# A four-layer graph kernel: the adjacency matrix is kept as two fp16 parts instead of being split again in each layer

## The chip, the cores and the metric

The kernel runs on one core of a Trainium2 chip. The time is the device time of one execution in microseconds (us), and a version's time is the median of its runs. The profile is of one execution, and its span is the time from that execution's first to its last instruction.

## The reference

`x` is 4096x128, `adj` is 4096x4096, both fp32. `adj` has about 0.2% of its entries and the diagonal set, and each row is divided by its count. Four layers follow each other, each with a residual and a layer norm:

```
x = LN(x + L0(x, adj))   XW = mobius(W, x); g = 2/(1-|XW|^2); (adj @ (g*XW)) / (adj @ (g-1)), then row-wise artanh, tanh
x = LN(x + L1(x, adj))   d^-1/2 (adj + I) d^-1/2 @ x @ W.T + b
x = LN(x + L2(x, adj))   dis*adj*dis @ x - x + sigmoid(alpha) * (softmax(beta * cos(x, x) * adj) @ x - x)
x = LN(x + L3(x, adj))   m = relu(adj @ x @ Wm.T + b); GRU cell of m and x
```

So `adj` (64 MB) multiplies a 4096x128 matrix four times, and layer 2 forms a second 4096x4096 matrix of attention weights.

## The kernel before

TensorE needs `adj` with the contracted index on the partitions, so `adj` must be turned. The work is cut into 8 slabs of 512 rows (`SLABS`), each into 32 blocks of 128 columns; two blocks are a pair, four are a group. The fp32 products are made in the format fp32r in three parts: an operand v is split into a high part (a copy rounded to fp32r) and a low part (v minus high), and high x high, high x low and low x high are added up.

**Layer 0.** For each of the 128 pairs: SP loads a tile (`load_tile`), TensorE turns 8 squares into a PSUM strip (`turn0`, two strips, run `AHEAD` = 4 pairs ahead), ScalarE copies the strip to SBUF (`full0`, a ring of 3 groups) and from there makes the high part (`high0`), VectorE subtracts to get the low part (`low0`), and TensorE multiplies both parts, as weights, with `Y` (`multiply0`, 16 products, 8 of 260 columns and 8 of 130). SP stores the turned fp32 strips in `adj_t` in DRAM. The result of a slab lands in four PSUM banks; `read_acc0` takes it out at the fourth pair of the next slab, and `rows0` does the row-wise arithmetic of a slab (scale, artanh, tanh, layer norm; some 40 small steps listed in `ROWS[0]`, spread over ScalarE, VectorE and GpSimd, each waiting for the one before by a semaphore) during the next slab. `Y` itself is also split in two parts: ScalarE's `y_high`, GpSimd's `y_low`.

**Layers 1 and 3.** SP loads groups of `adj_t` (`load_group`, 6 places, 1 MB each); for each pair ScalarE makes the high part (`high`, L857) and VectorE the low part (`low`, L1446), and TensorE makes 6 products of 512 columns (`multiply`, L541, L542, L550). The first 32 pairs take slabs 0 and 1 in turns (`TURNS`), because the last groups of `Y` come late. Row work (`rows1`, `rows3`) follows each slab. It puts small fp32 products on TensorE. The identity of layer 1 is added by four products with `eye`.

**Layer 2.** TensorE makes the scores of 32 row blocks (`score`, fp16, 3 products per half unit), VectorE multiplies them by `adj` (`mask`, which loads `adj` again in units of 0.5 MB), ScalarE takes the exponentials and scales them. 39 steps behind, TensorE turns the weights block by block (`turn2`), VectorE adds `dis` times the block of `adj_t` (`mix`, L1528), ScalarE and GpSimd (some on VectorE) split the sum (`high2`, `low2`), and TensorE makes 3 products (`multiply2`, L619 to L622).

**What sets the order.** Each engine's program is a written list and runs strictly in order; semaphores tie them. Row work is placed between pairs at fixed positions (`ROWS_FROM`, `HOOKS`, and leads `ACT_LEAD`, `DVE_LEAD`). All loads and the `adj_t` stores are in SP's queue, in order. There, the units that overwrite `x_nat` (places 22 to 25) wait until all of layer 2's `Y` is ready, and what stands behind them waits too.

Of the kernel before, what the change touches and what calls it, by code (L numbers as in the profile page):

```python
# [7 lines left out]
F32R = mybir.dt.float32r  # L8
# [25 lines left out]
LOADS = 14  # L34

# [3 lines left out]
AHEAD = 4  # L39
FULL_SLOTS = 3  # L40
# [41 lines left out]
KEPT_SLOTS = 4  # L82
# [4 lines left out]
     "floor_clip", "artanh_a", "artanh_b", "ratio", "h4", "log", "dcol", "dis", "series", "differ", "choose",  # L87
# [23 lines left out]
def build(nc, x, adj, w0, w1, b1, alpha, beta, w_msg, b_msg, w_ih, w_hh, b_ih, b_hh, out, scratch, dis_out):  # L111
    with ExitStack() as ctx:
# [6 lines left out]
        adj_t = nc.dram_tensor("adj_t", (SLABS, P, NB, SLAB), F32, kind="Internal").ap()  # L119
# [16 lines left out]
        Y = sb("Y", [P, NB, YW], F32R)  # L136
        part_h = sb("part_h", [P, 8, SLAB], F32R)
        part_l = sb("part_l", [P, 8, SLAB], F32R)
# [4 lines left out]
        turned_in = arena[:, TILE:FULL].rearrange("p (n w) -> p n w", w=Q * SLAB)  # L143
        full = arena[:, FULL:XNAT].rearrange("p (n w) -> p n w", w=Q * SLAB)
# [33 lines left out]
        dcol = sb("dcol", [P, NB])  # L178
        dis = sb("dis", [P, NB])
# [10 lines left out]
        scal = sb("scal", [P, 7])  # L190
# [5 lines left out]
        consts = sem("consts")  # L196
        dve_link = sem("dve_link")
# [24 lines left out]
        full_done = sem("full_done")  # L222
        stored = [sem(f"stored{n}") for n in range(FULL_SLOTS)]
# [5 lines left out]
        y_hi = sem("y_hi")  # L229
        y_ready = sem("y_ready")  # L230
# [46 lines left out]
        def parts_free(l, n):  # L277

            return product_base[l] if n < 4 and l > 1 else product_base[l] + n - 3
# [12 lines left out]
        def low_by_dve(b):  # L292
            return b in BY_DVE

        def low_at(l, n):
            if l == 2 and low_by_dve(n):
                return low_by_turns, BY_DVE.index(n) + 1
            skipped = len(BY_DVE) if l == 3 else sum(i < n for i in BY_DVE) if l == 2 else 0
            return low_done, product_base[l] + n - skipped + 1
# [1432 lines left out]
```

## Time and profile before

| what | value |
|---|---|
| median of 3 runs | 1412.92 us (1411.5 to 1417.08) |
| span of the profiled execution | 1412.7 us (no time of it is given apart from the span) |
| TensorE, VectorE, ScalarE, GpSimd busy | 93%, 77%, 75%, 41% of the span |
| DRAM read and written | 340 MB and 71 MB, 291 GB/s over the span |
| a copy of a 128x1024 strip, PSUM to SBUF, ScalarE (L802) | 1.01 us |
| four row squares with their sums, ScalarE (L833, L846) | 1.2 us; four relu (L841) 1.25 us; a change of function table 1.28 us |
| powers of 128x4 on GpSimd (L1096, L1098, L1103, L1106) | 1.0 to 1.1 us each |
| two wide GpSimd operations before the statistics (L1109, L1111) | 1.16 and 2.15 us |
| statistics of four blocks, VectorE (L1344 to L1351) | 1.4 us; four scalings (L1358) 1.1 us |
| two readouts of `acc0`, VectorE | 0.8 us |
| load of 0.5 MB of `adj` (L408), issue to landing | 5.9 us median |

A line of the windows view gives the stretch and its length, then for TensorE's products, its weight loads, VectorE, ScalarE and GpSimd the busy us and the number of instructions, then the granted TensorE clock as a share of full speed, the busy share of the 16 DMA engines, and GB/s. A line of a timeline gives start, length, engine, line of code, operation, result and operands; in brackets how long the engine was idle before it and what ended that. Products are pipelined, so the distance between starts is what one costs, not its length.

### The profile page before, as it was taken

The numbers are of one execution on the slowest core, as the hardware profiler recorded it, in microseconds if no ns is written. First come the engines' busy times: TensorE is split into PE (matmuls) and PEld (weight loads), VectorE is DVE, ScalarE is ACT, GpSimd is POOL, SyncE is SP. The second block draws the span as 40 slices with busy tenths as digits, with TensorE's granted clock in tenths as the row PEclk, the third lists the DMA queues.
The fourth block names the chain that finished last, engine by engine and source line by source line (L and its number), as shares of the span: only waits on it lengthen the run. The fifth ranks groups of instructions, "written<-read, shape, count | busy, mean of one in ns | idle before, by whom it ended". The sixth has DMA issues, their size and how long they took to land.

```text
span 1412.7 us, 21062 instructions
## 1 busy us (share of the span) xinstructions
PE 1308.7 (93%) x7640; PEld 1016.7 (72%) x7640; DVE 1085.0 (77%) x1946; ACT 1059.0 (75%) x1367; POOL 579.1 (41%) x441
## 2 busy tenths in 40 slices
PE   6999999999988989998799999999999879999996
PEld 5999999999986767773466666666666658767664
DVE  6856556555767989998888887988888878787885
ACT  6887888788777667775688879788798547767764
POOL 4312222222563543343477767777776650000010
PEclk9999999999989999999899999999999999999998
DMA  9999999999967878893678778788786849877860
GB/s 310 408 370 361 332 359 376 330 347 353 352 234 252 314 255 323 327 375 148 254 276 307 267 268 318 264 295 293 248 315 219 280 174 403 321 273 261 291 222 22
DMA packets 114824, 413.08 MB, mean 292 GB/s; under 512 B 10016, under 2 KB 23584, under 8 KB 90144
## 3 DMA queue, kind: packets, MB, share of 16 engines
q1 hardware_dynamic: 106528, 407.67, 79.3%
q10 hardware_dynamic: 8192, 4.06, 1.0%
q8 instruction: 60, 0.98, 0.3%
q14 instruction: 44, 0.36, 0.1%
HBM read 340.40 MB, written 71.30 MB: 291 GB/s over the span
## 4 chain that ended last, share of the span: by engine, by line
PE 53%; DVE 19%; ACT 16%; issue 7%; POOL 5%; DMA 1%; POOLq 0%; ACTq 0%; DVEq 0%; SPq 0%
DVE part_l L1446 6%; PE strip_b L605 5%; PE acc L550 5%; PE acc L541 4%; PE acc L542 4%; PE acc L522 3%; PE mid L522 3%; ACT arena L802 3%; PE acc L622 3%; PE strip_b L502 2%; DVE part_l L1325 2%; PE acc L619 2%; PE acc L620 2%; ACT part_h L857 2%; PE strip_a L502 2%
## 5 line engine op out<-in xcount | busy, mean ns | idle before, releaser
L1446 DVE TENSOR_TENSOR part_l<-arena,part_h 128x1024 fp32r<-128x1024 f32 x256 | 327.4, 1314 | 60.8 <-ACT part_h L857 59.4
L1150 POOL TENSOR_TENSOR part_l<-arena,part_h 128x512 fp32r<-128x512 f32 x237 | 304.4, 1298 | 151.0 <-ACT part_h L895 151.0
L857 ACT ACTIVATE part_h<-arena 128x1024 fp32r<-128x1024 f32 x256 | 265.7, 1057 | 125.6 <-PE acc L550 116.5
L1325 DVE TENSOR_TENSOR part_l<-arena,part_h 128x1024 fp32r<-128x1024 f32 x128 | 160.9, 1266 | 121.9 <-ACT part_h L809 121.1
L895 ACT ACTIVATE part_h<-arena 128x512 fp32r<-128x512 f32 x256 | 157.9, 625 | 94.8 <-DVE arena L1528 94.2
L541 PE MATMUL acc<-part_h,Y 128*128 128x512 f32 x512 | 222.2, 434 | 4.3 <-DVE arena L1333 2.1
L542 PE MATMUL acc<-part_h,Y 128*128 128x512 f32 x512 | 204.6, 400 | 0.0
L1118 POOL TENSOR_TENSOR sc<-sc,power 128x4 f32<-128x4 f32 x31 | 48.4, 1560 | 318.5 <-DVE sc L1351 318.5
L605 PEld LDWEIGHTS strip_b<-ident,arena 128*128 128x128 f32 x1024 | 126.1, 142 | 71.5 <-DVE arena L1528 20.1
L550 PE MATMUL acc<-part_l,Y 128*128 128x512 f32 x512 | 165.6, 405 | 10.3 <-DVE part_l L1446 10.1
L605 PE MATMUL strip_b<-ident,arena 128*128 128x128 f32 x1024 | 156.1, 275 | 18.8 <-DVE arena L1528 11.7
L809 ACT ACTIVATE part_h<-arena 128x1024 fp32r<-128x1024 f32 x128 | 135.8, 1061 | 35.5 <-PE mid L522 33.2
L522 PE MATMUL acc<-Y,part_h 128*128 128x260 f32 x496 | 143.3, 340 | 0.0
L522 PE MATMUL mid<-Y,part_h 128*128 128x260 f32 x496 | 142.7, 338 | 0.0
L884 ACT ACTIVATE arena<-arena,neg_peak 128x2048 f32<-128x2048 f32 x64 | 127.5, 1993 | 5.3 <-DVE neg_peak L1498 5.3
L520 PE MATMUL acc<-Y,part_l 128*128 128x130 f32 x512 | 126.4, 247 | 0.0
L550 PEld LDWEIGHTS acc<-part_l,Y 128*128 128x128 f32 x512 | 95.6, 191 | 39.2 <-DVE part_l L1446 18.4
L541 PEld LDWEIGHTS acc<-part_h,Y 128*128 128x128 f32 x512 | 98.2, 192 | 35.3 <-issue 7.9
L619 PE MATMUL acc<-part_h,Y 128*128 128x512 f32 x256 | 122.1, 477 | 0.0
L542 PEld LDWEIGHTS acc<-part_h,Y 128*128 128x128 f32 x512 | 98.0, 191 | 29.3 <-issue 9.1
L890 ACT ACTIVATE arena<-arena,weight 128x2048 f32<-128x2048 f32 x57 | 113.6, 1994 | 6.2 <-DVE weight L1512 6.2
L520 PE MATMUL mid<-Y,part_l 128*128 128x130 f32 x512 | 115.9, 226 | 0.0
(296 smaller groups left out, 2782.2 us busy)
## 6 DMA issues: line engine op xcount, KB each, us to landing
arena<-adj_t SPq DMA_DIRECT2D x128, 1024.0 KB, 4.9
arena<-in_adj SPq DMA_DIRECT2D x64, 1024.0 KB, 8.8
adj_t<-arena SPq DMA_DIRECT2D x64, 1024.0 KB, 8.0
arena<-in_adj SPq DMA_DIRECT2D x128, 512.0 KB, 5.9
part_h<-adj_t SPq DMA_DIRECT2D x64, 512.0 KB, 5.1
part_l<-adj_t SPq DMA_DIRECT2D x64, 512.0 KB, 5.1
scratch<-v ACTq DMA_DIRECT2D x8, 256.0 KB, 10.6
arena<-scratch SPq DMA_DIRECT2D x8, 256.0 KB, 5.3
```

Of the source, the lines that this page charges most:

```text
L520: last = pe.matmul(acc0[q][:, 0:LO], part_l[:, slot, mine], Y[:, j, 0:LO], start=False, stop=False)
L522: last = pe.matmul(acc0[q][:, 0:YW], part_h[:, slot, mine], Y[:, j, :], start=False, stop=stop)
L541: pe.matmul(to, Y[:, j, 0:D], h, start=j == 0, stop=False)
L542: pe.matmul(to, Y[:, j, LO:LO + D], h, start=False, stop=False)
L550: last = pe.matmul(to, Y[:, j, 0:D], part_l[:, 2 * (n % 4) + j % 2, :], start=False, stop=j == NB - 1)
L605: last = pe.transpose(strip_b[:, b % 2, P * q:P * (q + 1)], unit_in[:, place, P * (j % 8):P * (j % 8 + 1)], ident[:])
L619: pe.matmul(to, Y[:, j, 0:D], part_h[:, b % 4, :], start=j == 0, stop=False)
L857: act.activation(flat(part_h[:, slot:slot + 2, :]), turned_pair(n), ACT.Copy).then_inc(high_done, 1)
L895: act.activation(part_h[:, b % 4, :], mixed[b % G_SLOTS], ACT.Copy).then_inc(high_done, 1)
L1150: pool.tensor_tensor(part_l[:, b % 4, :], mixed[b % G_SLOTS], part_h[:, b % 4, :].bitcast(F32), ALU.subtract).then_inc(low_done, 1)
L1325: dve.tensor_tensor(flat(part_l[:, slot:slot + 2, :]), full_pair(n), flat(part_h[:, slot:slot + 2, :]).bitcast(F32), ALU.subtract).then_in ...
L1446: dve.tensor_tensor(flat(part_l[:, slot:slot + 2, :]), turned_pair(n), flat(part_h[:, slot:slot + 2, :]).bitcast(F32), ALU.subtract).then_ ...
```

## The change

`adj_t` becomes fp16 and holds for each block the high part and the low part of 1024 x `adj`, so its size stays. The copy `full0` goes: ScalarE's `high0` and VectorE's `low0` read the PSUM strip and write the two fp16 parts into a ring of 7 groups, from which TensorE multiplies and SP stores. `AHEAD` is 2, and a strip is free when `low0` has read it. Layers 1 and 3 multiply the loaded parts; `high` and `low` are gone there. In layer 2 `mix` takes only the high part of `adj_t`, and a fourth product multiplies the low part with `Y_dis`, a new fp16 matrix (`dis` times x). `Y` is fp16 too. Scale factors keep fp16 in range. `y_low` of layers 2 and 3 becomes two GpSimd instructions, in layer 2 `y_with_dis` is a third; in layer 0 `y_low0` is on VectorE, and `sum_parts` and `sum_den` move from GpSimd to VectorE. Two steps, `dcol_y` and `dis_y`, are added to `ROWS[0]` on GpSimd.

```diff
-AHEAD = 4
-FULL_SLOTS = 3
+A_SCALE = 1024.0
+AHEAD = 2
+RING_SLOTS = 7
-KEPT_SLOTS = 4
+KEPT_SLOTS = 6
...
-        adj_t = nc.dram_tensor("adj_t", (SLABS, P, NB, SLAB), F32, kind="Internal").ap()
+        adj_t = nc.dram_tensor("adj_t", (SLABS, GROUPS, P, Q * 2 * SLAB), F16, kind="Internal").ap()
-        Y = sb("Y", [P, NB, YW], F32R)
+        Y = sb("Y", [P, NB, YW], F16)
+        Y_dis = sb("Y_dis", [P, NB, D], F16)
...
# SP: stores, reloads of a pair for layer 2
-                    sp.wait_ge(full_done, 2 * n + 2)
+                    sp.wait_ge(low_done, 2 * n + 2)
+                    sp.dma_start(adj_t[s, c], ring_slot(n)).then_inc(stored[n % RING_SLOTS], 16)
-                    sp.wait_ge(mixed_done, 2 * (n - KEPT_SLOTS) + 2)
+                    sp.wait_ge(product, product_base[2] + 2 * (n - KEPT_SLOTS) + 2)
...
# TensorE: turn0, multiply (layers 1 and 3), multiply2
-                    pe.wait_ge(full_done, n - 1)
+                    pe.wait_ge(low_done, n - 1)
+                    high, low = pair[:, j % 2, 0, :], pair[:, j % 2, 1, :]
+                    pe.matmul(to, Y[:, j, 0:D], high, start=j == 0, stop=False)
+                    pe.matmul(to, Y[:, j, LO:LO + D], high, start=False, stop=False)
+                    last = pe.matmul(to, Y[:, j, 0:D], low, start=False, stop=j == NB - 1)
...
+                pe.matmul(to, Y_dis[:, j, :], kept_slot(b // 2 % KEPT_SLOTS)[:, b % 2, 1, :], start=j == 0, stop=False)
...
# ScalarE
-            def full0(n):
-                act.activation(full_pair(n), flat(strip[n % 2][:]), ACT.Copy).then_inc(full_done, 1)
             def high0(n):
-                act.activation(flat(part_h[:, slot:slot + 2, :]), full_pair(n), ACT.Copy).then_inc(high_done, 1)
+                if g >= RING_SLOTS:
+                    act.wait_ge(*held_stored(g - RING_SLOTS))
+                    act.wait_ge(product, 2 * (g - RING_SLOTS) + 2)
+                act.activation(ring_pair(n)[:, :, 0, :], strip[n % 2][:], ACT.Copy, scale=A_SCALE).then_inc(high_done, 1)
...
-                high(1, n)
-                high(3, n)
...
# GpSimd
             def y_low(l, g):
+                source = mx[:, rows_, :]
+                if l > 1:
+                    pool.wait_ge(y_ready, SLABS * l + g)
+                    source = turned[0][:].rearrange("p (q d) -> p q d", d=D)
+                    pool.tensor_scalar(source, x_nat[:, rows_, :], Y_SCALE, 0.0, ALU.mult, ALU.add).then_inc(x_scaled, 1)
+                    pool.wait_ge(x_scaled, SLABS * (l - 2) + g + 1)
+                pool.tensor_tensor(Y[:, rows_, LO:LO + D], source, Y[:, rows_, 0:D], ALU.subtract).then_inc(y_ready, 1)
+            def y_with_dis(g):
+                pool.tensor_tensor(Y_dis[:, rows_, :], x_nat[:, rows_, :], wide(dis_y[:, rows_]), ALU.mult)
...
                 if 6 <= n < 6 + GROUPS:
+                    y_with_dis(n - 6)
                     y_low(2, n - 6)
...
# VectorE
+            def y_low0(g):
+                dve.scalar_tensor_tensor(Y[:, rows_, LO:LO + D], Y[:, rows_, 0:D], -Y0_LOW, mx[:, rows_, :],
+                                         ALU.mult, ALU.add).then_inc(y_ready, 1)
             def low0(n):
+                dve.scalar_tensor_tensor(pair[:, :, 1, :], strip[n % 2][:], A_SCALE, pair[:, :, 0, :],
+                                         ALU.mult, ALU.subtract).then_inc(low_done, 1)
-                low(1, n)
-                low(3, n)
```

## Rows read from the trace of the kernel before

**Rows 1.** windows of the four layers; columns as in the section on the profile
```profile
38.00:418.50 380.50, 360.51 (x3035) 354.89 (x3033) 228.22 (x475) 309.82 (x451) 112.31 (x90) 0.97 0.94 348
418.50:641.50 223.00, 208.79 (x934) 163.90 (x935) 200.23 (x301) 152.73 (x194) 90.28 (x51) 0.97 0.83 308
641.50:1150.00 508.50, 474.19 (x2584) 304.26 (x2582) 430.20 (x838) 395.75 (x468) 345.09 (x276) 0.99 0.76 267
1150.00:1390.00 240.00, 231.99 (x916) 167.40 (x917) 189.55 (x244) 168.76 (x204) 13.55 (x10) 0.99 0.72 265
```

**Rows 2.** timeline of TensorE in layer 1 (start, us, what); five products lie between
```profile
571.27 0.39 PE L541 MATMUL acc<-part_h,Y 128*128 128x512 f32 x1
...
572.66 0.39 PE L541 MATMUL acc<-part_h,Y 128*128 128x512 f32 x1
```

**Rows 3.** timeline of TensorE in layer 2, around one block
```profile
866.73 0.60 PE L605 MATMUL strip_b<-ident,arena 128*128 128x128 f32 x4
867.08 0.47 PE L619 MATMUL acc<-part_h,Y 128*128 128x512 f32 x1
867.40 0.39 PE L620 MATMUL acc<-part_h,Y 128*128 128x512 f32 x1
...
868.09 0.38 PE L589 MATMUL strip_a<-arena 128*128 128x512 f16 x1
868.30 0.38 PE L590 MATMUL strip_a<-arena 128*128 128x512 f16 x1
```

**Rows 4.** timeline of TensorE in layer 0: transposes of successive pairs
```profile
85.16 1.04 PE L502 MATMUL strip_b<-ident,arena 128*128 128x128 f32 x8
...
87.88 1.03 PE L502 MATMUL strip_a<-ident,arena 128*128 128x128 f32 x8
```

**Rows 5.** chain that ended last: like marks, six slabs apart, then one slab apart
```profile
86.51 1.23 DVE part_l L1325
...
371.80 1.23 DVE part_l L1325
...
765.81 1.28 DVE arena L1487
...
825.85 1.28 DVE arena L1487
```

**Rows 6.** a window of layer 0 with dense transfers
```profile
50.00:55.00 5.00, 5.00 (x46) 5.00 (x45) 5.00 (x4) 4.56 (x6) 2.66 (x2) 1.00 1.04 416
```

**Rows 7.** timeline of SP's queue where layer 3 begins
```profile
1145.93 20.01 SPq L424 DMA_DIRECT2D arena<-scratch  x2
```

**Rows 8.** groups by line: count, busy us, mean ns, idle before and its releaser
```profile
L809 ACT ACTIVATE part_h<-arena 128x1024 fp32r<-128x1024 f32 x128 | 135.8, 1061 | 35.5 <-PE mid L522 33.2
...
L520 PEld LDWEIGHTS acc<-Y,part_l 128*128 128x128 f32 x512 | 100.7, 197 | 0.0
...
L1528 DVE SCALAR_TENSOR_TENSOR arena<-part_l,dis,strip_b 128x512 f32<-128x512 f32 x128 | 93.8, 742 | 9.0 <-PE strip_b L605 4.8 <-DMA part_l<-adj_t 3.5 <-issue 0.5
...
L588 PEld LDWEIGHTS strip_a<-arena 128*128 128x128 f16 x128 | 12.4, 97 | 41.0 <-issue 29.2 <-DVE peak L1487 10.5
```

**Rows 9.** timeline of VectorE in slab 0 of layer 0, two like instructions
```profile
34.03 0.69 DVE L1319 TENSOR_TENSOR arena<-arena,v 128x512 f32<-128x512 f32 x1
...
35.77 1.76 DVE L1319 TENSOR_TENSOR arena<-arena,v 128x512 f32<-128x512 f32 x1
```

**Rows 10.** timelines of GpSimd, SP, VectorE where layer 2 begins, one line group
```profile
650.18 1.04 POOL L1146 TENSOR_TENSOR v<-arena,sc 128x512 f32<-128x512 f32 x1
651.18 9.89 POOL L1078 TENSOR_TENSOR Y<-arena,Y 128x512 fp32r<-128x512 f32 x8
...
661.10 5.68 SPq L408 DMA_DIRECT2D arena<-in_adj  x9
...
672.56 1.28 DVE L1487 CUSTOM_DVE_ANT_0 arena<-strip_a,arena,scal 128x1024 f32<-128x1024 f32 x1
...
L1168 POOL TENSOR_SCALAR v<-v,scal 128x512 f32<-128x512 f32 x8 | 5.6, 694 | 0.1
```

More of the change, by code:

```diff
@@ L34 @@
 LOADS = 14
-AHEAD = 4
-FULL_SLOTS = 3
+A_SCALE = 1024.0
+Y0_SCALE = 0.25
+Y0_LOW = 2048.0
+Y_SCALE = 256.0
+WHOLE = A_SCALE * Y_SCALE
+AHEAD = 2
+RING_SLOTS = 7
 TURNED_SLOTS = 6
@@ L293, in low_by_dve, with low_at @@
             return b in BY_DVE
[L295 to L299, printed above, removed]
+        def low_at(b):
+            if low_by_dve(b):
+                return low_by_turns, BY_DVE.index(b) + 1
+            return low_done, split_done(b) - sum(i < b for i in BY_DVE)
         def unit_loads(k):
@@ L403, in load_unit @@
                         last = (GROUPS * SLABS - 1 - slot) // TURNED_SLOTS * TURNED_SLOTS + slot
-                        sp.wait_ge(low_done, product_base[1] + 2 * last + 2)
+                        sp.wait_ge(product, product_base[1] + 2 * last + 2)
                     else:
@@ L517, in multiply0 @@
                         mine = slice(P * q, P * (q + 1))
+                        high, low = pair[:, j % 2, 0, mine], pair[:, j % 2, 1, mine]
                         if start:
-                            pe.matmul(acc0[q][:, 0:YW], part_h[:, slot, mine], Y[:, j, :], start=True, stop=False)
-                        last = pe.matmul(acc0[q][:, 0:LO], part_l[:, slot, mine], Y[:, j, 0:LO], start=False, stop=False)
+                            pe.matmul(acc0[q][:, 0:YW], high, Y[:, j, :], start=True, stop=False)
+                        last = pe.matmul(acc0[q][:, 0:LO], low, Y[:, j, 0:LO], start=False, stop=False)
                         if not start:
-                            last = pe.matmul(acc0[q][:, 0:YW], part_h[:, slot, mine], Y[:, j, :], start=False, stop=stop)
+                            last = pe.matmul(acc0[q][:, 0:YW], high, Y[:, j, :], start=False, stop=stop)
                 last.then_inc(product, 1)
@@ L824, in read_acc @@
                     act.wait_ge(row[s % 2], row_base(1, s))
-                act.activation(to, acc[:, s % 2, :], ACT.Copy).then_inc(acc_read, 1)
+                act.activation(to, acc[:, s % 2, :], ACT.Copy, scale=1.0 / WHOLE).then_inc(acc_read, 1)
             def rows0(k, s):
@@ L1101, in rows0 @@
                     pool.tensor_tensor(dcol[:, mine], sc[:, DEG, :], sc[:, KEEP, :], ALU.mult).then_inc(row[par], 1)
+                    before("dcol_y")
+                    pool.tensor_scalar(dcol_y[:, mine], dcol[:, mine], Y_SCALE, 0.0, ALU.mult, ALU.add).then_inc(row[par], 1)
                     before("dis")
                     pool.tensor_tensor(dis[:, mine], sc[:, ZERO, :], inv_half[:, 0:Q], ALU.pow).then_inc(row[par], 1)
+                    before("dis_y")
+                    pool.tensor_scalar(dis_y[:, mine], dis[:, mine], Y_SCALE, 0.0, ALU.mult, ALU.add).then_inc(row[par], 1)
                 if k == 20:
@@ L1371, in rows0 @@
                 total = nat[:, :, D + 1]
+                if k == 7:
+                    before("sum_parts")
+                    dve.wait_ge(acc_read, acc_reads_done(0, s))
+                    dve.scalar_tensor_tensor(t_of[par][:], nat[:, :, LO:LO + D], 1.0 / Y0_LOW, nat[:, :, 0:D],
+                                             ALU.mult, ALU.add).then_inc(row[par], 1)
+                    before("sum_den")
+                    dve.scalar_tensor_tensor(val(DEN), nat[:, :, LO + D], 1.0 / Y0_LOW, nat[:, :, D],
+                                             ALU.mult, ALU.add).then_inc(row[par], 1)
                 if k == 8:
@@ L1646, in _ @@
                 low0(n)
+                if s == 0 and 1 <= m <= GROUPS:
+                    y_low0(m - 1)
                 if s > 0:
```

190 lines of the change are left out of this document (90 added, 100 removed).

## The prediction

> **What bounds the kernel now.** I read the stages first, then in each the engine that is never idle, then what it waits for. [rows 1] cut the span at the layer boundaries: layer 0 takes 380.5 us, layer 1 223, layer 2 508.5, layer 3 240, the tail 22.7. TensorE is busy 94 to 97% of each, so the spacing of its instructions decides most of it. In layers 1 and 3 the reader is to see six fp32r products of 512 columns per pair of blocks in 1.39 us (0.232 each, [rows 2]). In layer 2 one block takes 0.35 for four transposes, 0.32 for the first product, then 0.23 each, while the fp16 score products follow at 0.215 [rows 3]. Layer 0 takes 2.72 us per pair when nothing waits [rows 4]; that is about 0.8 of transposes (0.35 for four, [rows 3]) and 1.9 for 16 short products. But six of its slabs take 285.3 us between like marks, 47.5 each [rows 5], which is 4 us more than 16 x 2.72: the row work of the slab before holds ScalarE up. A slab of layer 2 takes 60.04 us [rows 5], 2.4 more than 32 blocks of 1.80.
>
> **Layer 1.** The split of `adj` goes: one 1.06 us ScalarE and one about 1.3 us VectorE instruction per pair, 128 times each in this layer, so that no compute engine feeds TensorE. What is late next is TensorE itself, since 6 fp16 products take 6 x 0.2155 = 1.293 us. A slab is 16 x 1.293 = 20.7 plus 2.1 for 20 small fp32 products (eye, weight, unit) at about 0.1, as four transposes take 0.35 in [rows 3], 22.8 us. A slab of transfers is 8.39 MB; at the 416 GB/s of [rows 6] it takes 20.2 us, so it stays hidden, by 2.6 us per slab. Sum: 8 x 22.8 = 182.4, 1 to start, and about 5 at the start for the last row work of layer 0 and for `x_bias` of slabs 1 and 2: the former is a chain like that of the next paragraph but one with `Y` behind it, about 33 us, and pair 28 (28 x 1.293 = 36) needs its end. 189 against 223: **-34**, bounds -24 to -44.
>
> **Layer 3.** The same saving per pair is 0.1 us; its row work is TensorE's own and stays. 116 pairs after the first 12 give -12. The first 12 have their data early; the next groups wait in SP's queue behind the reload of the last `scratch` slab, which held it for 20 us [rows 7]. That slab's layer norm no longer shares VectorE with four 1.2 us subtractions, so SP goes on some 3 us earlier: **-15**, bounds -6 to -20.
>
> **Layer 0.** ScalarE loses one of two 1 us copies per pair. Products get half-width weights: the load takes 97 ns instead of 197 [rows 8], and two loads of about 0.117 make the 0.235 us in which a product of 130 and one of 260 columns follow each other. With fp16 390 columns at 2.4 GHz take 0.163; I take 0.175, so a pair costs 0.8 + 8 x 0.175 = 2.2 us instead of 2.72 (bounds 2.1 and 2.72). This would be 35 us a slab. It is not what I predict, because the strip now holds more: `AHEAD` falls from 4 to 2, and a strip is free only when VectorE too has read it. So TensorE's transposes of pair n+2 wait for `low0(n)`, and what is queued behind `high0` and `low0` on ScalarE and VectorE is the row work of the slab before, 42 steps with hand-overs. I added up that row work between `low0` of pair 4 and of pair 15 from the small durations in the table of the profile section and 0.2 for each step on VectorE, with 1.06 for `high0` [rows 8] and 1.22 to 1.28 for `low0` (0.742 for 512 columns from PSUM [rows 8] and 512 more at the same rate). Pair 4: 3.6 us (low, degrees, then a wait of 1.3 for four squares); pair 5: 3.4 (two powers on GpSimd); 6: 1.7; 7: 3.2 (Ln, then four GpSimd instructions where two stood; the new two of 128x4 I take at 0.3 each, between nothing and the 0.69 of a 128x512 one, [rows 10]); 8: 2.0; 9 and 10: 4.9 (relu, squares, power, tanh); 11: 4.0; 12: 4.9 (3.3 on GpSimd before the statistics); 13: 3.2; 14 and 15: 1.2 each. This makes 33.3. At the slab's end TensorE turns pair 18, and its first product waits until high0(18), low0(18) and the readout behind them are done (1.06 + 1.28 + 0.8 + hand-overs, 3.3 us), a stall that 4 pairs ahead had covered. From low0(14) to the next low0(4): two pairs of 2.2, 1.0, 3.3, 1.4, one pair of 2.2, a transpose group of 1.0 and 1.1, 14.4 us. Slab: 33.3 - 1.2 + 14.4 = 46.5 against 47.5. Sum over seven slabs -7. In slab 0 the subtraction of `Y` leaves GpSimd, which had slowed VectorE's `y_scale` from 0.69 (the first, when GpSimd was idle) to 1.77 [rows 9]; low, scale and the new `y_low0` make 2.65 a pair against 2.83, and 2.2 for the rest: -3 with the new stall at its end. **-10**, bounds -40 and +15.
>
> **Layer 2, begin.** GpSimd now prepares `Y` in three instructions per group instead of one. Before, eight took 9.9 us [rows 10]. Now each group is 1.04 (like the product with a wide operand), 0.69 (tensor_scalar) and 1.24, with hand-overs 3.1, so 24.6: `y_ready` is 14.7 us later. SP stops for it and then issues nine units and the first pairs, as it did at 661.1. The first of those units is used by the mask at 672.6 [rows 10]; it would land at 661.1 + 14.7 + 5.9 (such a load's median, in the table) = 681.7. So the cover of 672.6 - 661.1 - 5.9 = 5.6 us is used up and **+9** is left (bounds +3 and +14). SP's queue also has the pairs behind it: first pair at 675.8 + 10 x 0.524 MB / 0.41 + 2 = 690.6, when the first mix is ready for it.
>
> **Layer 2, steady.** One product more per block, 0.2155. Three others shorten by 0.017, and the first after the transposes by 0 to 0.1. TensorE's block becomes 1.86 to 1.95, I take 1.895, +0.095 or 3.0 per slab. A part of the 2.4 us of waits shrinks, as the other engines gain 3 us of slack per slab: +2.2 a slab over 6.8 slabs. **+15**, bounds 0 and +32. In the last 39 steps (no scores) VectorE and GpSimd set the pace; six times 0.75 us more on GpSimd in that chain: **+3** (0 to +5). Pairs are reloaded only after their product, but with 6 places instead of 4, so a load is asked for at the same step.
>
> **Sum.** -34 - 15 - 10 + 9 + 15 + 3 = -32. The profiled execution spans 1412.7, the median of the runs is 1412.92 and I know of no time of that execution outside its span. Prediction 1381.
>
> *Two rules of the Trainium skill.* The 416 GB/s of [rows 6] is above what the Trainium skill ("DMA: Bandwidth & Descriptors", Specifications) calls the limit of HBM for one core, about 358 GB/s; by that rule a slab of layer 1 would take 8.39 / 0.358 = 23.4 and one of layer 0 46.9, some 8 us more in all; this trace disagrees in all its dense stretches. The fp16 products of 512 columns follow at 0.215 in [rows 3]; "TensorE: Matmul & The Clock Gate" of the Trainium skill (Back-to-back issue gap) gives about 131 ns in a sustained stream, by which layer 1 would be bound by transfers at 20.2 a slab, 21 us less, 1360 in all; the rows disagree, and I give it 0.02.
>
> **Rivals.** (B) The waits of layer 0 hide each other, and transfers become its bound: 16.78 MB a slab at 0.41 is 41 us, 5.5 less than I have, seven times: 1381 - 38 = 1343. For it: ScalarE has 1 us less per pair. Against it: the chain is serial across three engines. 0.15. (C) Transfers of layers 0 and 1 don't hold 410 GB/s beside TensorE's faster pace (most of layer 0 shows 350 to 380): at 358 it costs 8: 1389. 0.1. (D) Layer 2 pays in full, the new product costs 0.316 as the first one does and no wait shrinks: 32 x 0.145 = 4.6 a slab, +31, and the begin +14: 1402. 0.14. (E), the other side: the strip loop of layer 0 is serial. If row work, transposes, high and low of a strip don't overlap with the other strip's, a pair costs 0.95 + 1.06 + 1.28 + 0.2 = 3.5 us, a slab 56: +8.5 seven times instead of -1, +67: 1447. It decides from a slab of about 52.5 us on (47.5 + 33/7, with its -7 given back). For it: both strips wait on one VectorE. Against it: only what exceeds 2.2 us per pair shows. 0.06. A last one: fp16 weights load no faster, a pair stays at 2.72, which shows only in the five steps without row work, 2.5 a slab: 1400, 0.08. My forecast has 0.45.
>
> Range 1350 to 1404: its low end leaves most of B out, the high end leaves E. Alone my forecast would be 1366 to 1394. Within 0.5% of 1412.92 (1405.9 to 1420) is what a measurement can't tell from no change. Slower 0.07 (E and a sum of bounds), same 0.08, faster 0.85.
>
> **What would show it.** Slabs of layer 0: 46 to 47 us between marks, and TensorE waiting on VectorE's low instead of ScalarE's copy. Layer 1: TensorE's spacing 0.215, slabs near 22.8, no DVE or ACT beside. Layer 2: slabs near 62.2; a gap of VectorE of 7 us before mask 16, ended by a transfer. The forecast is wrong if layer 0's slab is under 44 or over 50, if a transfer ends TensorE's waits in layer 1, or if layer 2's slab is over 64.

## The result, and the profile after

| | us |
|---|---|
| before, median of 4 runs | 1415.0 (1411.5 to 1418.4) |
| after, median of 4 runs | 1367.3 (1362.4 to 1371.9) |
| ratio | 0.966, 95% interval 0.962 to 0.971 |
| forecast | 1381, range 1350 to 1404 |
| span of the profiled execution, before and after | 1412.7 and 1361.2 |

The four runs of after lie in two groups, 1362.4 and 1363.0, and 1371.6 and 1371.9; the profiled execution belongs to the first. The experiments point to the reason.

The first block has the windows of the four layers after the change, with the columns of [rows 1]. The second has the kernel before once more for layers 1 and 3 alone, cut from the layer's first product to its last, and a stretch near the start of its layer 3. The third has after, cut in the same way:

```profile
38.00:398.80 360.80, 305.82 (x3055) 277.49 (x3054) 221.34 (x494) 182.67 (x324) 69.41 (x83) 0.96 0.96 365
398.80:585.80 187.00, 187.00 (x943) 95.71 (x944) 38.09 (x178) 29.51 (x73) 50.67 (x50) 1.00 0.96 363
585.80:1123.50 537.70, 510.55 (x2831) 298.02 (x2829) 426.77 (x838) 398.28 (x466) 335.86 (x299) 0.98 0.72 255
1123.50:1361.00 237.50, 223.00 (x948) 103.85 (x948) 51.82 (x149) 49.20 (x89) 12.84 (x14) 0.98 0.72 272
```

```profile
418.50:638.60 220.10, 205.89 (x917) 161.94 (x918) 199.25 (x300) 151.79 (x192) 90.28 (x51) 0.97 0.83 308
1151.30:1393.60 242.30, 235.58 (x928) 169.66 (x929) 191.82 (x247) 168.76 (x204) 12.85 (x9) 0.99 0.71 261
...
1165.00:1170.00 5.00, 5.00 (x13) 3.96 (x12) 5.00 (x5) 3.70 (x4) 0.00 (x0) 0.50 0.68 247
```

```profile
398.80:582.00 183.20, 183.20 (x918) 92.81 (x919) 37.25 (x177) 27.44 (x68) 50.67 (x50) 1.00 0.95 362
1123.50:1342.40 218.90, 216.63 (x929) 101.08 (x930) 43.05 (x119) 43.52 (x78) 10.83 (x12) 1.00 0.77 293
```

The reader is to see that layer 1 has become TensorE alone: busy 183.20 of 183.20 us, VectorE down from 199 to 37, clock 1.00. In layer 0 TensorE's busy time fell by 55 us, but the layer's by 20 only, so something else sets its pace there. Layer 2 is longer and TensorE busier.

TensorE's timeline in layer 1 and around one block of layer 2, against [rows 2] and [rows 3]:

```profile
499.79 0.38 PE L567 MATMUL acc<-arena,Y 128*128 128x512 f16 x1
500.01 0.38 PE L568 MATMUL acc<-arena,Y 128*128 128x512 f16 x1
500.23 0.38 PE L574 MATMUL acc<-arena,Y 128*128 128x512 f16 x1
...
501.09 0.38 PE L567 MATMUL acc<-arena,Y 128*128 128x512 f16 x1
...
860.48 0.60 PE L629 MATMUL strip_b<-ident,arena 128*128 128x128 f32 x4
860.91 0.38 PE L643 MATMUL acc<-parts,Y_dis 128*128 128x512 f16 x1
861.13 0.38 PE L644 MATMUL acc<-parts,Y 128*128 128x512 f16 x1
...
861.78 0.38 PE L612 MATMUL mid<-arena 128*128 128x512 f16 x1
```

Six products take 1.30 us (1.39 before). A block of layer 2 is 0.43 for the transposes and seven products at 0.2155, 1.94 us (1.80 before). The four transposes and the product behind them take 0.67 before and 0.65 after: most of what the first product no longer costs (0.22 instead of 0.32) the transposes take instead (0.43 instead of 0.35). So of the "0 to 0.1 less" for that product only 0.02 came, and the block came out at the upper end of 1.86 to 1.95.

The end of a slab in layer 0, after: the low part of pair 2 and the read-out behind it on VectorE, then TensorE's first product of the next slab, once at slab 2 and once at slab 3, with windows of the clock behind each.

```profile
123.58 1.22 DVE L1352 SCALAR_TENSOR_TENSOR parts<-strip_a,parts 128x1024 f16<-128x1024 f32 x1 [0.99 <-ACT parts L828]
124.72 0.42 DVE L1359 TENSOR_SCALAR arena<-mid 128x260 f32<-128x260 f32 x1
125.06 0.42 DVE L1360 TENSOR_SCALAR arena<-mid 128x260 f32<-128x260 f32 x1
125.62 0.38 PE L543 MATMUL acc<-Y,parts 128*128 128x260 f16 x1 [3.13 <-DVE arena L1360]
...
170.97 0.27 PE L543 MATMUL acc<-Y,parts 128*128 128x260 f16 x1 [3.13 <-DVE arena L1360]
```

```profile
125.60:128.00 2.40, 2.38 (x16) 1.93 (x17) 0.00 (x0) 0.00 (x0) 0.00 (x0) 0.50 1.02 384
128.00:130.00 2.00, 2.00 (x19) 1.95 (x17) 0.00 (x0) 0.41 (x1) 0.00 (x0) 0.78 0.92 380
...
171.00:174.00 3.00, 3.00 (x34) 2.84 (x35) 0.00 (x0) 0.62 (x1) 0.00 (x0) 1.00 1.04 414
```

TensorE waits 3.13 us each time, the "3.3 us stall" of the forecast. What the forecast didn't have is the granted clock behind it: 0.50 after the first of the two (2.4 GHz has become 1.2), 1.00 after the second, though the wait is the same. In this execution the clock falls so behind five of the seven waits at slab ends.

Two marks in a slab of layer 0, VectorE's low part of pair 4 and of pair 15, first in slab 3 of before, then in slab 3 of after. Between them lies the row work of the slab before: 35.05 us, and 29.26 us.

```profile
181.61 1.22 DVE L1325 TENSOR_TENSOR part_l<-arena,part_h 128x1024 fp32r<-128x1024 f32 x1 [1.12 <-ACT part_h L809]
...
216.66 1.22 DVE L1325 TENSOR_TENSOR part_l<-arena,part_h 128x1024 fp32r<-128x1024 f32 x1
```

```profile
176.66 1.22 DVE L1352 SCALAR_TENSOR_TENSOR arena<-strip_a,arena 128x1024 f16<-128x1024 f32 x1 [0.19 <-ACT arena L828]
...
205.92 1.21 DVE L1352 SCALAR_TENSOR_TENSOR parts<-strip_b,parts 128x1024 f16<-128x1024 f32 x1
```

The start of layer 2, against [rows 10]. On GpSimd one group of `Y` is three instructions; SP goes on when the last is done; VectorE's mask 16 and the first mix are ended by transfers.

```profile
594.32 1.04 POOL L1101 TENSOR_TENSOR Y_dis<-arena,dis_y 128x512 f16<-128x512 f32 x1
595.33 0.62 POOL L1095 TENSOR_SCALAR turned<-arena 128x512 f32<-128x512 f32 x1
596.04 1.17 POOL L1097 TENSOR_TENSOR Y<-turned,Y 128x512 f16<-128x512 f32 x1
...
619.78 1.16 POOL L1097 TENSOR_TENSOR Y<-turned,Y 128x512 f16<-128x512 f32 x1
620.96 4.31 SPq L428 DMA_DIRECT2D arena<-in_adj  x9
625.01 1.28 DVE L1517 CUSTOM_DVE_ANT_0 arena<-strip_a,arena,scal 128x1024 f32<-128x1024 f32 x1 [5.79 <-DMA arena<-in_adj]
637.57 1.41 DVE L1558 SCALAR_TENSOR_TENSOR arena<-parts,dis,strip_b 128x512 f32<-128x512 f16 x2 [2.17 <-DMA parts<-adj_t]
```

GpSimd needs 26.6 us instead of 9.9, and VectorE waits 5.79 us for the first unit behind it (7 were forecast).

### The profile page after: what moved, and what is told of

Read it like the earlier page. It is cut to its first block, busy times and chain, and to the rows that moved or that the text cites. A ratio compares the mean times of both kernels' runs of the same rounds, so it can differ in the third digit from the quotient of the medians.

```text
span 1361.2 us, 20730 instructions
## 1 busy us (share of the span) xinstructions
PE 1245.8 (92%) x7896; PEld 793.4 (58%) x7896; DVE 762.8 (56%) x1716; ACT 680.2 (50%) x983; POOL 483.6 (36%) x459
## 4 chain that ended last, share of the span: by engine, by line
PE 72%; DVE 11%; ACT 6%; POOL 5%; issue 4%; DMA 2%; POOLq 0%; ACTq 0%; DVEq 0%; SPq 0%
PE acc L567 8%; PE acc L568 8%; PE acc L574 8%; PE strip_b L629 8%; PE acc L647 4%; PE acc L644 4%; PE acc L645 4%; PE acc L643 4%; DVE parts L1352 3%; PE strip_b L525 2%; PE strip_a L525 2%; DVE arena L1352 2%; PE strip_a L612 2%; PE strip_a L613 2%; PE strip_a L614 2%
## 5 line engine op out<-in xcount | busy, mean ns | idle before, releaser
L1170 POOL TENSOR_TENSOR parts<-arena,parts 128x512 f16<-128x512 f32 x237 | 275.2, 1170 | 190.0 <-ACT parts L908 186.6
L908 ACT ACTIVATE parts<-arena 128x512 f16<-128x512 f32 x256 | 158.5, 624 | 110.4 <-DVE arena L1558 101.7
L1558 DVE SCALAR_TENSOR_TENSOR arena<-parts,dis,strip_b 128x512 f32<-128x512 f16 x256 | 188.8, 743 | 29.6 <-PE strip_b L629 20.7
L567 PE MATMUL acc<-arena,Y 128*128 128x512 f16 x512 | 194.1, 379 | 3.5 <-DMA arena<-adj_t 2.5
L568 PE MATMUL acc<-arena,Y 128*128 128x512 f16 x512 | 194.1, 379 | 0.0
L574 PE MATMUL acc<-arena,Y 128*128 128x512 f16 x512 | 194.1, 379 | 0.0
L629 PE MATMUL strip_b<-ident,arena 128*128 128x128 f32 x1024 | 155.4, 275 | 7.2 <-ACT arena L903 4.8
L1517 DVE CUSTOM_DVE_ANT_0 arena<-strip_a,arena,scal 128x1024 f32<-128x1024 f32 x64 | 82.0, 1281 | 35.1 <-PE strip_a L614 29.3
L647 PE MATMUL acc<-parts,Y 128*128 128x512 f16 x256 | 97.1, 379 | 3.4 <-POOL parts L1170 3.4
L643 PE MATMUL acc<-parts,Y_dis 128*128 128x512 f16 x256 | 97.1, 379 | 0.1
L645 PE MATMUL acc<-parts,Y 128*128 128x512 f16 x256 | 97.0, 379 | 0.0
L644 PE MATMUL acc<-parts,Y 128*128 128x512 f16 x256 | 97.0, 379 | 0.0
L1517 DVE CUSTOM_DVE_ANT_0 arena<-mid,arena,scal 128x1024 f32<-128x1024 f32 x60 | 76.9, 1282 | 35.0 <-PE mid L614 35.0
L525 PE MATMUL strip_a<-ident,arena 128*128 128x128 f32 x512 | 68.9, 279 | 22.6 <-DVE parts L1352 14.4
L567 PEld LDWEIGHTS acc<-arena,Y 128*128 128x128 f16 x512 | 50.1, 98 | 66.5 <-issue 10.2
L568 PEld LDWEIGHTS acc<-arena,Y 128*128 128x128 f16 x512 | 50.1, 98 | 65.4 <-issue 12.6
L525 PE MATMUL strip_b<-ident,arena 128*128 128x128 f32 x512 | 71.2, 284 | 17.3 <-DVE parts L1352 9.8
L574 PEld LDWEIGHTS acc<-arena,Y 128*128 128x128 f16 x512 | 50.1, 98 | 59.5
```

Of the source, the lines that this page charges most:

```text
L525: last = pe.transpose(strip[n % 2][:, j % 2, P * q:P * (q + 1)], tile[:, j // Q, q, P * (j % Q):P * (j % Q + 1)], ident[:])
L567: pe.matmul(to, Y[:, j, 0:D], high, start=j == 0, stop=False)
L568: pe.matmul(to, Y[:, j, LO:LO + D], high, start=False, stop=False)
L574: last = pe.matmul(to, Y[:, j, 0:D], low, start=False, stop=j == NB - 1)
L629: last = pe.transpose(strip_b[:, b % 2, P * q:P * (q + 1)], unit_in[:, place, P * (j % 8):P * (j % 8 + 1)], ident[:])
L643: pe.matmul(to, Y_dis[:, j, :], kept_slot(b // 2 % KEPT_SLOTS)[:, b % 2, 1, :], start=j == 0, stop=False)
```

## The experiments

Each starts from one of the two kernels; the diff shows what it changes. Times are medians of 4 or 5 runs where a ratio is given, otherwise of one run. A ratio is to runs of the kernel before that were taken beside it.

In layer 0, "low n" is VectorE's low part of pair n of a slab (0 to 15). A "gap" is the time from the start of one low part to the start of the next, and "a slab takes" is the time from one low 0 to the next. The "first mix" is VectorE's first `mix` of layer 2.

**Read-out one pair earlier.**

```diff
 # ScalarE's and VectorE's loops of layer 0
-                if m == 3 and s > 0:
+                if m == 2 and s > 0:
                     read_acc0(s - 1)
```

> The changed kernel with one edit: in layer 0 the read-out of a slab's sums stands one pair earlier in ScalarE's and VectorE's queues (before the copies of pair 2 of the next slab instead of behind them). Theory (the stall at the slab's end is 3.13 us of waiting for the read-out, plus in every second slab 1.6 us of half clock after it): the gap from the low part of pair 2 to that of pair 3 falls from 5.5 and 7.1 us to about 3.5, a slab from 44.8 to 42.2, seven slabs -18, total about 1349. Rival 1 (the read-out now stands before VectorE's low part of pair 2 and delays it as much as it frees): -8 at most, 1359. Rival 2 (transfers already bound the slab at about 44): no change, 1367.

Measured: 1339.5, ratio to before 0.946 (0.942 to 0.949), 27.8 less than the changed kernel. VectorE's low part of pair 0 in two successive slabs, and the clock over one of them:

```profile
115.37 1.23 DVE L1352 SCALAR_TENSOR_TENSOR parts<-strip_a,parts 128x1024 f16<-128x1024 f32 x1 [1.18 <-ACT parts L828]
...
156.96 1.22 DVE L1352 SCALAR_TENSOR_TENSOR parts<-strip_a,parts 128x1024 f16<-128x1024 f32 x1 [1.17 <-ACT parts L828]
...
157.00:198.60 41.60, 37.06 (x387) 33.69 (x385) 26.79 (x67) 23.05 (x42) 7.94 (x10) 1.00 1.03 416
```

A slab takes 41.6 us, the gap from low 2 to low 3 is 3.3 instead of 5.5 to 7.1 (up to 7.6 in other runs with after's layer 0), in slabs 2 to 5 every other gap is unchanged to 0.02 us, and the clock is 1.00. The theory has the place right and the size too small (-18 expected). The seven gaps together are 22.4 us shorter than in the profiled execution of after, 3.2 each where 2.6 were expected: the clock had fallen behind five of its seven waits, not behind every second. Most of the rest is that this execution of after lay 4.3 us under its kernel's median. Transfers reach 416 GB/s, so rival 2 falls.

**The wait filled.** The kernel after with this:

```diff
                 if m == 0 and s > 0:
+                    pe.wait_ge(low_done, n + 2)
+                    for _ in range(24):
+                        pe.transpose(strip[(n + 1) % 2][:, 0, 0:P], ident[:], ident[:])
                     pe.wait_ge(acc_read, acc_reads_done(0, s - 1))
```

> The changed kernel with TensorE's wait at each slab's end in layer 0 filled: 24 transposes into the strip that is free then, results unused (overwritten by the next transposes), 2.6 us of the 3.1. The wait for the read-out itself stays. Theory (half clock after the idle stretch is what makes the gap from low 2 to low 3 7.1 to 7.6 us in most slabs instead of 5.5): all gaps 5.5, slab 43.8, layer 0 up to its end 363 less 3, total about 1357, and its runs lie closer together. Rival (the clock falls for another reason, as the total load): gaps of 7 or more stay, 1365.

Measured: 1353.3 (1351.3 to 1354.0), ratio 0.954 (0.953 to 0.956). Slabs 1 to 5 take 43.7 us each, gap 2 to 3 is 5.4 in all of them, and the clock is 1.00:

```profile
119.00:162.70 43.70, 39.83 (x411) 36.25 (x409) 26.78 (x66) 22.93 (x43) 7.94 (x10) 1.00 1.02 392
```

Useless work made the kernel 14 us faster than the changed kernel's median (the kernel before took 1418.1 beside it, 3 us more than beside the changed kernel). So the theory holds (1357 expected), and the runs do lie closer together, within 2.6 us. The idle stretch itself is not what differs between the slabs of after, since it is 3.13 us in all; whether the clock falls behind it is. With after's layer 0, a slab with no fall takes 43.8, with one 45.2 to 46.7. From the first low part to the start of layer 1 this run takes 355.2 us, the profiled run of after 363.0, and three other profiled runs with this same layer 0 (the three below that leave layer 0 alone) 371.3 to 371.6. In those three the clock falls behind all seven waits. That difference, 8.4 us, is about the distance between the two groups of runs of after, 9.0. So the fall of the clock is the likely reason for the two groups; no execution of the slower group of after was profiled.

Windows of the run with `Y_dis` in layer 1, which is one of the three; in it both slabs lose clock behind the stall:

```profile
117.50:164.30 46.80, 40.04 (x388) 35.99 (x386) 26.84 (x67) 22.97 (x43) 7.94 (x10) 0.93 0.99 363
164.30:209.70 45.40, 38.63 (x386) 34.99 (x384) 26.74 (x66) 22.95 (x42) 7.95 (x10) 0.96 0.99 367
...
172.00:174.00 2.00, 2.00 (x13) 1.80 (x12) 0.00 (x0) 0.00 (x0) 0.00 (x0) 0.50 1.03 417
```

**The look-ahead in the kernel before.**

```diff
-AHEAD = 4
+AHEAD = 2
...
+                if m == 3 and s > 0:
+                    read_acc0(s - 1)
                 full0(n)
-                if m == 3 and s > 0:
-                    read_acc0(s - 1)
                 high0(n)
```

> The kernel before with AHEAD = 2 instead of 4, and the read-out of a slab's sums moved ahead of the full-width copy of pair 3, which that needs. Nothing else of the change. Theory (the shorter look-ahead costs a stall at each slab's end and nothing in the row work, because there the row work's chain is the bound): slab 47.5 to about 50.5, +21, total about 1434. Rival 1 (look-ahead had also covered the row work): 3 us more per slab beyond that, +40, 1453. Rival 2 (look-ahead was worth nothing): 1414.

These are two edits: with the shorter look-ahead the read-out has to stand ahead of the copy. Measured: 1474.1, +60. A slab takes 54.6 instead of 47.5. From low 4 to low 15, where the row work lies, the eleven gaps add up to 35.0 in both, so look-ahead covers nothing there, and rival 1 is wrong about the place. The slab's end pays all 7 us: gap 2 to 3 is 8.8 instead of 3.2, and the gaps before it lose their head start (low 0 to low 1 is 3.35 instead of 2.05 or 2.73). The theory had the place and about a third of the size (+21). Part of what it lacked is once more the clock, 0.50 for a while behind TensorE's wait in every one of these slabs:

```profile
143.80 0.36 PE L519 MATMUL acc<-Y,part_h 128*128 128x260 f32 x1 [4.23 <-DVE arena L1333]
```

```profile
144.70:148.10 3.40, 3.40 (x17) 3.40 (x17) 0.00 (x0) 0.00 (x0) 0.40 (x2) 0.50 0.01 2
```

**Row work spread, loads halved.** Both with the earlier read-out. The first puts relu, squares, tanh and the layer norm of layer 0 into pairs of their own; the second adds that only half of each tile is loaded from slab 1 on.

```diff
+STEPS0 = {3: [7], 4: [8], 5: [9], 6: [10, 11], 7: [12, 13], 8: [14, 15, 16, 17], 9: [18], 10: [19], 11: [20, 21],
+          12: [22], 14: [24, 26], 15: [27]}
 # ScalarE, GpSimd, VectorE
-                    rows0(2 * m, s - 1)
-                    rows0(2 * m + 1, s - 1)
+                    for k in STEPS0.get(m, []):
+                        rows0(k, s - 1)
```

> The changed kernel with the earlier read-out and the row work of layer 0 spread over more pairs: steps 7, 8, 9 alone, relu and squares apart, the last steps in pairs 14 and 15. Theory (in the run with the earlier read-out alone both bounds lie together: row work gives 41.6 us a slab, transfers 40.9 at 0.41): a slab 41, total about 1335, and tile loads or stores end waits. Rival 1 (row work's chain is the only bound, transfers could go faster): the spread takes gaps of 3.6, 3.6 and 4.0 to about 2.6, a slab 39, total 1322. Rival 2 (the spread brings other convoys): 42.5, total 1346.

> As the run with the earlier read-out and the spread row work, but from slab 1 on only half of each tile of adj is loaded in layer 0 (the rest stays from slab 0, so the output is another). 12.6 MB a slab instead of 16.8. If transfers are the bound there: a slab falls from 41 to the engines' 38 to 39.5, total 15 to 20 below the run beside it. If they are not: a slab as in the run beside it, within 0.3 us.

Measured: 1327.3, ratio 0.938 (0.933 to 0.942), and 1326.6. One window of each, spread and then halved:

```profile
115.00:154.00 39.00, 35.77 (x376) 32.79 (x374) 25.91 (x66) 22.07 (x42) 7.95 (x10) 1.00 1.03 416
```

```profile
115.00:154.00 39.00, 35.77 (x376) 32.76 (x375) 26.19 (x66) 22.19 (x42) 7.94 (x10) 1.00 0.86 314
```

A slab takes 40.0 us in both, at 416 and at 314 GB/s. So the transfers are not the bound even at 40.0, where 16.78 MB need 419 GB/s. What remains is the row work's chain (gaps of 3.8, 3.4 and 3.6). The theory for the spread, that transfers hold the slab at 41, falls; its first rival is nearer, with less gain than it gave.

**The split of `adj` in layers 1 and 3 of the kernel before, cut to 8 of 1024 columns.**

```diff
-                act.activation(flat(part_h[:, slot:slot + 2, :]), turned_pair(n), ACT.Copy).then_inc(high_done, 1)
+                act.activation(flat(part_h[:, slot:slot + 2, :])[:, 0:8], turned_pair(n)[:, 0:8], ACT.Copy).then_inc(high_done, 1)
 # and the same on VectorE's subtraction
```

> The kernel before with the split of adj in layers 1 and 3 reduced to 8 of 1024 columns per pair (ScalarE's high and VectorE's low; the products use what the buffers still hold, so the output is another). Products stay fp32r, 0.232 apart. It separates the two sources of the gain in these layers. Theory: the faster products are 12.8 us in each layer (128 x 0.1), the rest is waits for the split: layer 1 from first to last product 220.1 falls to 196, layer 3 242.3 to 231.7, total about 1380. Rival (the fp16 transfers or something else of the change gave the rest): layer 1 above 205, layer 3 above 238.

Measured: 1378.2. First to last product of layers 1 and 3:

```profile
417.40:613.40 196.00, 195.69 (x917) 159.80 (x918) 63.54 (x300) 50.23 (x192) 51.96 (x50) 1.00 0.94 351
1126.40:1357.40 231.00, 229.37 (x929) 169.08 (x930) 61.81 (x247) 63.68 (x204) 9.98 (x10) 1.00 0.74 275
```

So layer 1's 36.9 us are 24.1 from the split and 12.8 of spacing; layer 3's 23.4 are 11.3 and 12.1. Both as expected to within 1 us. The expectation calls the split's share waits, but of the 24.1 only 13.9 are idle time of TensorE (14.2 before, 0.3 here). In the other 10.2 it was busy and slower, part of that at half clock (mean granted clock 0.97 before, 1.00 here). In layer 3 half of the 11.3 lies in the first eight pairs (19.2 us before, 13.4 here, 10.8 after), the rest behind the row work of later slabs.

**Layer 2 without its fourth product** (the line with `Y_dis` in `multiply2` left out, and the output with it less exact).

> The changed kernel with layer 2's fourth product (Y_dis by the stored low part) left out, so its output is less exact; all transfers and copies stay. It prices that product. Theory (TensorE alone sets layer 2's pace now, its block 1.945 us, but the other engines come next at 58 to 60 us a slab, as the kernel before showed 60.05 with a block of 1.80): a slab falls from 62.76 to about 59, -30, total about 1337. Rival 1 (TensorE is the only bound): a block of 1.73, slab 55.4, -58, total 1309. Rival 2 (the product hides beside waits): slab above 61.5, less than -10.

Measured: 1341.9. A slab takes 58.5 instead of 62.8, and TensorE is idle for 1.9 us of it:

```profile
700.00:758.40 58.40, 56.54 (x326) 33.87 (x324) 50.85 (x102) 49.68 (x58) 39.40 (x35) 1.00 0.82 292
```

The product costs 4.3 us a slab where its 32 x 0.2155 are 6.9; the rest comes back as waits. Its layer 0 was one of the long ones (371), so the comparison by layer is surer than the 25 us against the changed kernel's median: from the first mix to layer 3 it takes 453.9 instead of 486.0, 32 less.

**`Y_dis` in layer 1, and low `Y` on VectorE.** The first moves GpSimd's multiplication for `Y_dis` behind each slab's unit rows of layer 1; the second adds that layer 2's low part of `Y` is one VectorE instruction per group (and a wait each on SP and on GpSimd that this needs, not shown).

```diff
 # GpSimd, rows1, k == 8
                     pool.tensor_tensor(v[:], x_nat[:, mine, :], wide(sc[:, H, :]), ALU.mult).then_inc(row[par], 1)
+                    y_with_dis(s)
 # GpSimd, steps 6 to 13 of layer 2
-                    y_with_dis(n - 6)
                     y_low(2, n - 6)
```

```diff
 # VectorE, step 6 of layer 2, instead of GpSimd's y_low(2, g)
                     rows1(6, SLABS - 1)
+                    for g in range(GROUPS):
+                        y_low2(g)      # one scalar_tensor_tensor of 128x512
```

> The changed kernel with one edit: Y_dis, the operand of layer 2's fourth product, is made group by group on GpSimd in layer 1, as soon as the rows are there, instead of in the chain before y_ready. Theory (y_ready sets the start of layer 2 through SP's reloads, and the cover of 5.6 us is used up): y_ready comes 8 x 1.04 = 8.3 us earlier after the layer's boundary, the first mix 7 us earlier, total about 1360. Rival (the start is set by the transfers behind y_ready or by the scores, not by y_ready): first mix at most 2 us earlier, 1365 to 1367.

> The changed kernel with Y_dis made in layer 1 (as in the run before) and layer 2's low part of Y made by VectorE in one instruction per group instead of two on GpSimd. Theory (y_ready still sets the start: nine reloads and the first pairs wait behind it in SP's queue): y_ready about 20 us earlier after the boundary than with Y_dis in layer 1 (8 x 0.7 = 5.6 us of VectorE behind the last layer norm); then y_ready is early and the scores and masks set the first mix, which comes 42 to 46 us after layer 1's last products instead of 47.4: total 1355 to 1359. Rival (y_ready was the bound for all of it): first mix at 35, total 1348. Other side (VectorE's 5.6 us lie in the chain of the last slab's unit rows): first mix no earlier than 47, total 1361 or more.

Measured: 1360.8, ratio 0.961 (0.957 to 0.965), and 1369.8, ratio 0.967 (0.964 to 0.971). The profiled executions of both had the long layer 0. The first one's runs (1354.4 to 1364.8) overlap with the changed kernel's, so the comparison by layer is the surer one. From layer 1's last product to the first mix: 55.6 us in the changed kernel, 47.4 in the first (45.0 before), 53.7 in the second. Below is VectorE at the first mix in the one, and in the other the last five of its eight low `Y` and the unit rows' low part, which the scores wait for:

```profile
637.30 0.75 DVE L1558 SCALAR_TENSOR_TENSOR arena<-parts,dis,strip_b 128x512 f32<-128x512 f16 x1 [1.22 <-DMA parts<-adj_t]
```

```profile
599.66 4.78 DVE L1354 SCALAR_TENSOR_TENSOR Y<-arena,Y 128x512 f16<-128x512 f32 x5
...
612.25 0.69 DVE L1517 TENSOR_TENSOR arena<-mid,arena 128x512 f16<-128x512 f32 x1
```

In the first run that last instruction stands at 604.67, and layer 1 had ended there 0.4 us later. So moving 8.3 us off GpSimd gained the 8.2, and moving 14 more off it, onto VectorE, lost 6.3, by its "other side": there VectorE is the chain, and `y_ready` no longer (SP's reloads go out at 604.5, and the first mix is ended by TensorE, no longer by a transfer). In that run TensorE also waits 5.62 us for VectorE and then makes its first scores at granted clock 0.51 (605.6 to 611.0), which is part of the delay.

**Together.** Read-out, spread and both `Y` edits; then the same without the VectorE one.

> The changed kernel with three edits together: read-out one pair earlier, layer 0's row work spread over more pairs (relu, squares, tanh and the layer norm each in another pair's place), and Y_dis and low Y as in the run beside it. Theory (the gains add): 1339.5 from the earlier read-out, 1 less from the spread (transfers of 16.78 MB at 0.41 take 40.9 us of the 41.6 a slab has), 8 to 12 less from the start of layer 2: about 1328. Rival (the earlier stages don't add, since faster loads meet the same transfers): 1334.

> The changed kernel with the earlier read-out, the spread row work, and Y_dis made on GpSimd in layer 1; low Y of layer 2 stays on GpSimd (on VectorE it had delayed the masks). Theory (the two gains add, since one is layer 0's and the other layer 2's start): 1327.3 - 8 = 1319, layer 0's slabs 40.0, first mix 47 to 48 us after the last product of layer 1. Rival (the gain of the early Y_dis was that run's chance, as its verdict overlaps with the changed kernel's own runs): 1325 to 1328.

Measured: 1325.1, ratio 0.936 (0.933 to 0.940), and 1319.6 (1317.7 to 1322.3), ratio 0.931 (0.929 to 0.933), where 1328 and 1319 were expected. The last beats both kernels, the changed one by 48 us; its slabs take 40.0 and its first mix comes 47.1 us after layer 1's last product, as expected. Its windows of layer 0 and of layer 2:

```profile
36.00:362.60 326.60, 296.70 (x3056) 271.85 (x3056) 221.82 (x495) 181.59 (x324) 69.10 (x83) 0.98 1.01 406
...
546.10:1080.10 534.00, 511.07 (x2856) 299.82 (x2854) 426.18 (x840) 399.94 (x469) 326.22 (x292) 0.99 0.72 259
```

## Why the prediction was right, and where its sizes were off

| term | forecast | measured (profiled executions) |
|---|---|---|
| layer 0 | -10 | -19.7 here; -12 in three other runs |
| layer 1 | -34 | -36.9 |
| layer 2, begin | +9 | +10.6 |
| layer 2, steady | +15 | +19.3 |
| layer 2, end | +3 | -1.1 |
| layer 3 with tail | -15 | -23.7 |
| sum | -32 | -51.5 (median against median -47.7) |

Layer 2 is cut at its first mix and at the 39th mix before its last; the begin goes back to layer 1's last product, the end on to layer 3's first. Every term but the smallest has the forecast's sign, but the sizes differ. The measured 1367.3 is 14 us below the forecast, at the low edge of the narrower 1366 to 1394, and two of its four runs lie below that. In the profiled execution layers 0 and 3 gave 18 us more than forecast, layer 1 and the end of layer 2 gave 7 more, and the begin and the steady part of layer 2 cost 6 more.

**Layer 1.** Right by its own steps: spacing 0.2155, a slab 22.9 us from first to last product (22.8 forecast), no transfer ended a wait of TensorE (in layer 3 transfers ended 2.5 us of them). The forecast's extra 5 us for late rows at the start did not come; what hid this in the sum is that 189, which ends with the last product, was set against a window of 223 that goes 2.9 us beyond it.

**Layer 2.** The begin went as worked out, each link by about its size: GpSimd 16.7 us longer (14.7; six groups took 2.83 each where 3.1 were forecast, two took 4.8 beside VectorE's scaling), VectorE's gap 5.8 (7), ended by a transfer. The steady slab took 62.8, not 62.2; the block is 1.94, not 1.895, because transposes and first product together got only 0.02 cheaper. The kernel with three products confirms the other half of the step, that waits come back when TensorE gets shorter. Rival D had the full price in a block (0.145; measured 0.14) and is wrong in the slab: 4.6 us dearer by its sum, 2.7 in fact. The end was forecast 3 us dearer and took 1.1 less: that term was wrong, and it offset most of what the steady part cost beyond its +15. GpSimd's low part takes 1.17 us instead of 1.30 after the change (means of 237), which the forecast did not count; whether that is the reason was not tested.

**Layer 3.** The mechanism was right (spacing, and row work and first pairs freed from the split), the second term was mis-sized: spacing 12.1 (12), the end of the split 11.3 where the forecast had 3. Two things were missing. Before, the first pairs ran at half clock for a while (0.50 in the stretch shown from 1165 on) behind waits of 0.85 and 2.77 us, and were 5.8 us slower than without the split; and each later slab was some 0.8 us longer than without the split. TensorE's waits of 0.4 us for ScalarE in the row work of three slabs are gone without it, which fits row work that had waited behind the 1 us copies in ScalarE's queue; the rest of the 0.8 was not traced.

**Layer 0.** The step that failed is the size of the slab, 46.5. The steady slabs took 43.8 or 45.2 to 45.5 in the profiled execution of after, 45.5 or 46.7 in the three others. The forecast called itself wrong if a slab were under 44, and two of five are; its other signs held. The 46.5 were made of 32.1 for the row work (low 4 to low 15) and 14.4 for the slab's end (low 15 to the next low 4). Measured, the row work took 29.3 (35.0 before) and the end 14.5 to 17.4 (12.5 before).

The sum of the row work was off in both directions. It had too little for pair 6 (1.7; measured 2.7) and for pairs 9 and 10 together (4.9; 7.2). It had too much for pair 7 (3.2; 1.6), 11 (4.0; 1.4), 12 (4.9; 4.0) and 13 (3.2; 2.5). The relu and squares pairs, 9 and 10, fell from 4.6 and 4.7 to 3.6 each, about the 1 us of the copy that left ScalarE; no run took that copy away by itself. At the slab's end the half clock behind the stall adds up to 3 us that the sum did not have. The two errors have opposite signs, and by the clock's luck a run shows -12 or -20; only the first is near the forecast's -10. Slab 0 gave 2.7, near the 3 forecast, but not as worked out: four of its pairs with `Y` took 2.34 where 2.65 was forecast, and one took 4.7.

**The rivals.** B needed a slab of 41 and took transfers for its bound. The slab can be 40.0 and the transfers were not the bound at that; what kept after from it was the read-out behind pair 2 and row work bunched in few pairs. E is refuted: the two strips do overlap, gaps without row work are 2.21 us, against the 3.5 of a serial loop. The last one, that fp16 weights load no faster, is refuted too: a pair costs 2.21, not 2.72. C: the 363 to 388 GB/s in most slabs of layer 0, in after and in the run with `Y_dis` in layer 1, are demand, not a limit, as the same code with an earlier read-out shows 403 to 416.

*The rules of the Trainium skill.* "DMA: Bandwidth & Descriptors" (Specifications) has about 358 GB/s as one core's HBM limit; here, with this one core running the kernel, whole slabs of layer 0 run at 416, so the runs disagree. Of the 131 ns in "TensorE: Matmul & The Clock Gate" (Back-to-back issue gap) nothing was seen: the 768 products in each of layers 1 and 3 follow at 0.2155.

**Small slips** of the prediction, none of which moves its sum: 8 x 3.1 is 24.8, not 24.6; TensorE is busy 93%, not 94, in layer 2 before; [rows 9] has 1.76, not 1.77.

**What stays open.** What decides whether the clock falls behind one 3.13 us wait and not behind the next. Which pairs' row work got shorter by the copy that left, and why the end of layer 2 did. Whether the row work's chain could be brought under 40 us a slab was not tried.

## What to carry to other kernels

When a change shortens the look-ahead or moves a buffer's release, ask which single instruction per outer iteration the pipe now waits for, and try to place that instruction one step earlier: here one digit in each of two queues was worth 28 us. Price a stall by its idle time and by the slow stretch behind it. Work moved off a late engine helps until the engine that it is moved to becomes the chain: low `Y` on VectorE lost 6.3 us. Where an engine has idle time before a boundary, do the work there: `Y_dis` made in layer 1 gained 8.2 us.

## What the runs showed of the hardware

- Most of TensorE's 3.13 us waits at the slab ends of layer 0 were followed by 2.6 to 6.0 us at granted clock 0.50, some by none, in the same program. Profiled executions with the same layer 0 differed by 8.4 us in it. 24 transposes of no use in the wait kept the clock at 1.00 behind it and saved 14 us, median against median.
- Four fp32 transposes followed by an fp32r product take 0.35 + 0.32, followed by an fp16 product 0.43 + 0.22. A 512-column fp32 product before an fp32r one takes 0.46 and the next 0.63, before an fp16 one 0.86 and 0.22. The sums are 0.67 and 0.65, and 1.09 and 1.08, so at such a change of type fp16 weights gained next to nothing; in a steady stream they gained 0.017 a product.
- With GpSimd idle (no instruction there from 30 to 60 us), all eight `y_low0` took 0.68 us and all `y_scale` 0.68 to 0.69, where [rows 9] has 1.76 for the second `y_scale`. GpSimd's 1.04 and 0.62 us instructions took 2.02 and 1.59 beside VectorE's scaling of 128x2048 (at 608.5 and 616.1).
- One core moved 416 GB/s over whole slabs of 42 us, reads and writes mixed.
